# Two layers of cross attention and expert FFN on one core: the second score pass of each slot issued right behind the first on TensorE

## What is computed

```python
x = x + tanh(g_xattn[0]) * xattn0(layernorm(x), ctx)
x = x + tanh(g_ffn[0])   * ffn0(layernorm(x))      # 8 experts + 1 shared, top 4 of 8, silu gate, width 128
x = x + tanh(g_xattn[1]) * xattn1(layernorm(x), ctx)  # scores clipped to +-10000
x = x + tanh(g_ffn[1])   * ffn1(layernorm(x))      # 8 experts, top 2, relu, width 1024
# attention, 16 heads of 16:
q, k, v = heads(xn @ Wq + bq), heads(ctx @ Wk + bk), heads(ctx @ Wv + bv)
attn = softmax(q @ k.T * 16 ** -0.5)
out = merge(attn @ v) @ Wo + bo
```

## Time and profile before

| | |
|---|---|
| median of 3 runs | 1165.95 us (1160.27, 1165.95, 1166.85) |
| profiled execution | 1160.78 us, span 1159.0 us |
| PE matmuls busy | 957.9 us (83% of the span) |
| DVE busy | 768.1 us (66%) |
| ACT busy | 480.2 us (41%) |
| mean granted TensorE clock | 0.872 of full speed |

### The profile page before, as it was taken

How to read it: one execution, slowest core, us unless ns; L and a number is a source line. 1 busy time by engine, 2 the same in 40 slices (tenths; PEclk the granted TensorE clock), 3 DMA queues, 4 the chain that set the end, 5 groups by cost and what they waited for, 6 DMA issues and landing times.

```text
span 1159.0 us, 17921 instructions
## 1 busy us (share of the span) xinstructions
PE 957.9 (83%) x6385; PEld 758.5 (65%) x6385; DVE 768.1 (66%) x1607; ACT 480.2 (41%) x834; POOL 240.7 (21%) x389
## 2 busy tenths in 40 slices
PE   3578799999999899888897688782599799797993
PEld 2345577776767666656675455451599799797993
DVE  2544467757676677777777787754598588586681
ACT  1124444443434333323333333430367476475561
POOL 2011111010110010101000031110424344544443
PEclk9956899999999999899898665765599899899897
DMA  3985555054154161716267553230557665666552
GB/s 109 242 190 120 100 96 90 33 87 77 46 80 75 37 118 59 138 46 137 78 130 140 135 112 112 89 92 29 201 189 241 185 187 183 173 203 210 160 142 27
DMA packets 122055, 141.89 MB, mean 122 GB/s; under 512 B 11536, under 2 KB 106408, under 8 KB 121968
## 3 DMA queue, kind: packets, MB, share of 16 engines
q1 hardware_dynamic: 113136, 128.50, 44.7%
q0 software_dynamic: 8832, 12.25, 5.6%
HBM read 109.97 MB, written 30.75 MB: 121 GB/s over the span
## 4 chain that ended last, share of the span: by engine, by line
PE 36%; DVE 20%; issue 17%; DMA 11%; POOL 8%; ACT 5%; SPq 1%; POOLq 0%; DVEq 0%; ACTq 0%
DMA out_x<-x,token_i 8%; PE bank L752 6%; POOL out_x L1720 5%; DVE rowmax L1222 5%; PE value_bank L696 4%; PE bank L762 3%; DVE clipped L1247 3%; PE bank L723 3%; PE bank L607 3%; PE by_query L660 2%; PE bank L616 2%; PE by_key L681 2%; PE bank L646 2%; POOL xs_in L1707 2%; DVE x L1371 2%
## 5 line engine op out<-in xcount | busy, mean ns | idle before, releaser
L1222 DVE TENSOR_REDUCE rowmax<-by_query 128x4 f32<-128x1024 f32 x128 | 155.8, 1217 | 36.7 <-PE by_query L660 36.7
L1037 ACT ACTIVATE probs<-clipped 128x1024 f32<-128x1024 f32 x64 | 67.6, 1057 | 196.6 <-DVE clipped L1247 196.5
L1666 POOL TENSOR_SCALAR rstd<-moments 128x2 f32<-128x2 f32 x32 | 7.1, 223 | 591.4 <-DVE moments L1186 591.4
L1720 POOL DMA_INDIRECT out_x<-x,token_i x46 | 92.5, 2012 | 171.3 <-DMA out_x<-x,token_i 148.2
L912 PE MATMUL bank<-w_hi,h_hi 128*128 128x256 f32 x368 | 104.1, 283 | 0.0
L912 PE MATMUL bank<-w_lo,h_hi 128*128 128x256 f32 x368 | 104.1, 283 | 0.0
L912 PE MATMUL bank<-w_hi,h_lo 128*128 128x256 f32 x368 | 104.1, 283 | 0.0
L660 PE MATMUL by_query<-stack_k,stack_q 48*128 48x256 f32 x512 | 72.4, 365 | 33.8 <-DVE rowmax L1222 31.2
L660 PEld LDWEIGHTS by_query<-stack_k,stack_q 48*128 48x128 f32 x512 | 44.0, 212 | 76.1 <-DVE rowmax L1222 39.1
L681 PE MATMUL by_key<-stack_q,stack_k 50*128 50x256 f32 x512 | 69.6, 354 | 25.5 <-DVE clipped L1247 17.0
L696 PE MATMUL value_bank<-probs,values 128*32 128x256 f32 x1024 | 82.9, 450 | 7.8 <-ACT probs L1037 7.7
(11 more groups left out here) (237 smaller groups left out, 2252.4 us busy)
## 6 DMA issues: line engine op xcount, KB each, us to landing
w<-in_L_ffn_W SPq DMA_DIRECT2D x46, 1024.0 KB, 7.7
lower<-max SPq DMA_DIRECT2D x64, 256.0 KB, 3.4
stack_k<-qk SPq DMA_DIRECT2D x96, 128.0 KB, 5.0
stack_q<-qk SPq DMA_DIRECT2D x96, 128.0 KB, 7.4
qk<-hi SPq DMA_DIRECT2D x32, 256.0 KB, 4.1
qk<-lo SPq DMA_DIRECT2D x32, 256.0 KB, 4.6
rows<-w_gate SPq DMA_DIRECT2D x8, 264.0 KB, 3.9
x<-in_x SPq DMA_DIRECT2D x8, 256.0 KB, 6.7
```

The costliest lines, as they stand in the source:

```text
L1037: ac.activation(probs[i % 3][:, :, :, :].rearrange("p h k s -> p (h k s)"), src, ACT.Exp).then_inc(sem.exp_done, 1)
L1222: dv.tensor_reduce(rowmax[u % 2][:, 2 * p:2 * p + 2, :], by_query[:, :, :].rearrange("p h (t s) -> p h t s", t=TT), AX, ALU.max).then_inc( ...
L1720: po.indirect_dma_start(out[:, :], bass.IndirectOffsetOnAxis(ap=token_i[:, n:n + 1].bitcast(U32), axis=0), ysb[i % 3][:, t, :], None, comp ...
```

## The change

PE issues the key pass of a slot straight behind the query pass. The stages of the slot's first half come after both. The waits of both functions are as before, and so are the orders of all other engines.

```diff
@@ -843,12 +843,12 @@
             v, q = divmod(g - base(0), PAIRS)
             if 0 <= v < UNITS:
                 scores_by_query(v, q)
+            u, p = divmod(g - base(0) - LAG, PAIRS)
+            if 0 <= u < UNITS:
+                scores_by_key(u, p)
             for stage, n in PLAN[2 * g]:
                 if stage in stages:
                     stages[stage](n)
-            u, p = divmod(g - base(0) - LAG, PAIRS)
-            if 0 <= u < UNITS:
-                scores_by_key(u, p)
             u, p = divmod(g - base(0) - LAG - 2, PAIRS)
             if 0 <= u < UNITS and p % 2 == 0:
                 weigh_values(u, p // 2)
```

## The result

The changed kernel is slower: 1192.7 us in the median of four runs (1191.21 to 1194.57) against 1164.66 us, a ratio of 1.0245 with a 95% interval of 1.0213 to 1.0278. The forecast was 1161 us in a range of 1147 to 1177; the time is above even the rival that I had placed on that side (1180). The forecast was built on the profiled execution of before, 1160.78 us, which lies 3.9 under the median of before.

The account below looks back on a forecast made before the run. PE was taken as the bound from 197 to 412 us, taking turns with DVE from 412 to 637; 0 - 9.2 + 2.6 + 7.0 + 1.7 - 2.9 + 0 = -0.8 us on 1160.78, forecast 1161, range 1147 to 1177.

Parts of the forecast that it names:

- 22.1 us of PE time: Over the 77 slots with both score passes, fewer changes of form on PE save 22.1 us.
- -9.2 + 2.6: Slots 57 to 92: 9.2 us saved by fewer form changes, 2.6 us added by key passes waiting for exponentials.
- Up to slot 56: Half of 3.6 us saved, 1.8, set against 1.8 us of waits: 0.
- 0.4 x 17.5 = +7.0: Layer 1's ten late slots with a gate and up product: 0.4 of 17.5 us of waits stays, +7.0 us.
- The walk of slots 100 to 103: Thickest group of layer 1 waits, followed slot by slot: 2.7 us net for 6.7 us of waits, 0.4 each.
- +1.7 - 2.9: Layer 1: thirteen late slots without gate and up product cost +1.7 us; twenty slots outside the groups save 2.9.
- bounds -5.6 and +5.6, taken as 0: Seven slots at the end without query pass: passes shift by at most 0.80 us each, effect taken as 0.
- Rival (b): Layer 1 slower: clipping, key pass, first-half stages, tanh, products, clipping become one chain; +19 us, 1180; chance 0.15.
- Rival (a): Layer 1 swallows the new waits because PE stood waiting there anyway, savings count in full: 1145 us; chance 0.17.
- My own sign: In layer 1 the query pass waits for the maxima on DVE much less than 31.2 us.
- Rival (c): Layer 1's granted clock slides from 0.93 to 0.88 with PE idle in lumps, 11 us more work: 1170; chance 0.10.
- By program order alone: Matmuls start and end in order, so all 38.6 us of waits hold PE: 38.6 - 22.1 = +16.5, 1177.

Follow-up runs that it names:

- e10: Changed kernel with the exponential ahead of the first half's stages on ACT in layer 0 and the clipping ahead of them on DVE: 1131.85 us, ratio 0.9699.
- e4: Changed kernel with DVE clipping before the first half's stages of the slot, PE's order kept: 1155.22 us, ratio 0.9932 against the kernel before.
- e1: Kernel before, with the key pass ahead of the first half's stages only in layer 0's slots 29 to 92: ratio 1.001.
- e8: Kernel before, with the key pass ahead only in layer 1's 13 slots with a gate and up product in the first half: ratio 1.021.
- e9: Kernel before, with the key pass ahead only in layer 1's 20 query-pass slots without a gate and up product in the first half: ratio 0.998.
- e3: Kernel before, with the key pass ahead only in the last slots, 146 to 156 (also called e3_tail): ratio 1.0057.

## Why the prediction was wrong, point by point

- **The savings by change of form, "22.1 us of PE time",** were right in their prices: 0.34, 0.33 and 1.06 us between rows stand in the changed kernel's trace, and slots 57 to 92 show nearly the whole 9.2 us once nothing waits (e10, -8.7). But the sign that PE's busy time falls by about 20 us came only with the rings open (937.4 us in e10 and 939.6 in e4 for 957.9). In the changed kernel it was 957.1, 6.7 us less in slots 57 to 92 and 7.0 more in slots 146 to 156, which ran at the lower clock.
- **Layer 0, "-9.2 + 2.6".** Measured: -2.1. The waits were mis-sized. I held the end of the exponential in the old trace against the start of Q, and took all else as it stood. In slots 57 to 92 K waited 4.5 us for exponentials, not 2.6, and PE's idle time rose by 4.6; that each A behind a late K makes the next exponential late as well is how I read it. The other 2.5 us are savings that did not come (6.7 for 9.2). Up to slot 56, where I had set waits against half of the savings, it was +4.8 (e1: +4.2): K waited 2.0 us more there, near my 1.8, but PE's busy time did not fall (160.6 for 160.5 us), and why is open. Together K waited 14.5 us for exponentials in layer 0 after the change and 8.0 before, by the two rows here, before first:

```profile
PE by_key L681 <- ACT probs L1037: 8.0, 5, 2.7
```

```profile
PE by_key L681 <- ACT probs L1037: 14.5, 13, 2.6
```

- **Layer 1, "0.4 x 17.5 = +7.0".** This is the step that failed, with the largest miss (+15.7 in layer 1 for +5.8). The mechanism was named and its slots were the right ones (e8, e9), but the share of each wait that stays was half of what it is. By the starts of Q in the changed kernel, slot 93 made PE 4.1 us later, slots 100 to 104 3.8, slots 110 to 113 2.8 and slots 120 to 123 3.4: 14.0 us for the same 17.5 us of waits, 0.8 of each microsecond and not 0.4 (and +21.8 for these slots alone, e8). The waits as such were nearly right: K waits 62.8 us for its readers after the change and 25.0 before, 37.8 more where I had read 38.6. The walk of slots 100 to 103 failed in two places. It priced the products behind the wait at the full clock: from K's start to the next Q it is 4.85 us in the trace (468.14 to 472.99) for the walk's 3.2. And the 0.90 us that a bank wait was to give back were not given back: Q of slot 103 is 5.8 us later against before than Q of slot 100, where the walk said 2.7. Slot 104 gave part of it back, so that the group ends at 3.8, not far from 2.7. The larger mistake was to carry 0.4 from this group to the others: the wait of slot 93, read as 1.84 us, cost 4.1, since K waited 2.5 and the gate and up product behind it took 3.2 us for 1.9 at a granted clock of 0.59.
- **Layer 1's other slots, "+1.7 - 2.9".** Nothing speaks against it: -1.0 us and ratio 0.998 (e9), within what the stretch varies by.
- **The last slots, "bounds -5.6 and +5.6, taken as 0".** Wrong: +6.6, and +6.3 in e3, outside the bounds, of which up to 4 us may be the lower clock's (42.3 us for 38.4 in the order of before). I had priced one pass earlier or later, not that the router's products too stand behind a K that waits for the clipping, with DVE's router work ahead of that clipping: K's waits for it there went from 4.2 to 9.0 us. With the clipping first the stretch was 2.6 us shorter than before in e4 and 2.3 longer in e10, which is the width of the stretch.
- **Rival (b)** was the right one, with its place and chain, at a chance of 0.15 and a price of 19 us where the change cost 28; its sign, layer 1 longer by 15 us and more, came (+15.7). **Rival (a)**, waits that PE had anyway, fell with the row of Q's waits: 30.5 for 31.2. My own sign, that they get much shorter, fell with it. **Rival (c)**, the clock: its sign, below 0.9 from 412 to 637 us, did not come (0.91), and e3_tail at 0.92 lost 1.1 us in these slots. So the clock alone does not make the loss; behind the waits of the ring it made single slots longer (slots 93 and 100), and how much that is in all stays open.
- **By program order alone** the sum would have been 1177, closer than mine: to let every wait count in full was the better guess. It is still too low, and not for the waits (37.8 us more for 38.6), but because the 22.1 us that it takes off did not come off PE's busy time.

## What to carry to other kernels

When an instruction that waits is moved ahead of work that doesn't, draw the ring: does what it waits for stand, on its own engine, behind the results of the work now held back? If it does, count the waits read off the old trace nearly in full (here 0.8 of each microsecond in the slots with the gate and up product), and don't set savings against them that PE would only have if it did not wait. Move the reader forward on its engine together with the instruction on PE: here PE's move alone cost 2.45%, each reader's move alone gained nothing, and all three together gained 3.0%. And before a difference of one stretch is read as an effect, look how much that stretch varies in executions that have the same order there.

## What the runs showed of the hardware

Four fp32 matmul records of 256 columns (two in the program) between ordinary ones take 0.86 us, 0.10 more for each neighbour in the two-halves form, and 1.06 in front of the value pass, which uses 32 columns of the array. A wait of 1.48 us on PE was followed by matmuls at the lower clock (the down product 1.86 us in place of 0.96), and so was one of 2.4 us in slot 93; a wait of 1.26 us in the kernel before was not (0.97 us from the gate product's start at 476.69 to the up product's). The granted clock of slots 93 to 127 was 0.92 in one execution and 0.94 in three others that had the same order there, and the execution at 0.92 was no more than 1.1 us longer than any of them: in this stretch, where PE was idle for 27 to 32 us, the lower clock cost little. Three filler matmuls took 1.5 us and six 2.86 us.
